# Where the rows of the other view are fetched, where the 4-bit pieces stand, and where the final copy is issued

## What is computed

```python
x = x + _L0_attn_ref(_layernorm(x, axis=-1), L0_attn_weight_qkv, L0_attn_weight_out)
x = x + _L0_xattn_ref(_layernorm(x, axis=-1), ctx_2048, L0_xattn_Wq, L0_xattn_Wk, L0_xattn_Wv)
x = x + _L0_ffn_ref(_layernorm(x, axis=-1), L0_ffn_weight1, L0_ffn_weight2, L0_ffn_weight3)
...
x = x + _L3_ffn_ref(_layernorm(x, axis=-1), L3_ffn_gate_w, L3_ffn_w1, L3_ffn_w2, L3_ffn_w3)
return x
```

## Time and profile before

| | us |
|---|---|
| Median of 3 runs (lowest, highest) | 2310.97 (2307.03, 2313.88) |
| The profiled execution, its own time | 2306.32 |
| Its span in the trace | 2304.5 |
| attn0's PE work ends, xattn0's begins | 145.9, 150.3 |
| ffn0's PE work begins | 329.5 |
| Last indirect DMA of ffn3 issued | 2287.26 |
| Final copy issued | 2295.96 |

### The profile page before, as it was taken

How to read it: one execution, slowest core, us unless ns; L and a number is a source line. 1 busy time by engine, 2 the same in 40 slices (tenths; PEclk the granted TensorE clock), 3 DMA queues, 4 the chain that set the end, 5 groups by cost and what they waited for, 6 DMA issues and landing times. The chain is left out here.

```text
span 2304.5 us, 46693 instructions
## 1 busy us (share of the span) xinstructions
PE 2055.2 (89%) x18816; PEld 1569.9 (68%) x18816; DVE 1600.1 (69%) x2975; ACT 1238.0 (54%) x2456; POOL 302.9 (13%) x307
## 2 busy tenths in 40 slices
PE   7978989899899898888889998979889779999996
PEld 4654458677555787566656666768656658999996
DVE  5756657677465897888857877857566676766763
ACT  2325664545476444555546547655478524665653
POOL 0010000011310000010000000000100113444432
PEclk9979999999999999999989999999899879999998
DMA  3020010100100002000020000010200035667663
GB/s 121 22 66 23 14 44 1 37 1 1 60 20 25 11 1 73 1 1 1 1 81 1 9 18 0 0 37 1 73 2 2 15 112 185 211 194 222 195 208 89
DMA packets 59688, 125.70 MB, mean 55 GB/s; under 512 B 12968, under 2 KB 42281, under 8 KB 59337
## 3 DMA queue, kind: packets, MB, share of 16 engines
q1 hardware_dynamic: 50666, 110.96, 14.2%
q0 software_dynamic: 8832, 12.06, 2.5%
HBM read 108.79 MB, written 15.80 MB: 54 GB/s over the span
## 5 line engine op out<-in xcount | busy, mean ns | idle before, releaser
L268 PE MATMUL ps<-ffn_xh,ffn_wh 128*128 128x256 f32 x644 | 184.1, 286 | 1.5 <-DVE ffn_xl L4388 1.5
L268 PE MATMUL ps<-ffn_xh,ffn_wl 128*128 128x256 f32 x644 | 182.2, 283 | 0.0
L268 PE MATMUL ps<-ffn_xl,ffn_wh 128*128 128x256 f32 x644 | 182.1, 283 | 0.0
L4383 DVE TENSOR_TENSOR ffn_wl<-ffn_fresh,ffn_wh 128x1792 fp32r<-128x1792 f32 x69 | 139.4, 2023 | 26.5 <-ACT ffn_wh L4263 26.5
L216 POOL TENSOR_TENSOR all_rstd<-all_mv,all_cst 128x4 f32<-128x4 f32 x40 | 8.5, 212 | 1060.8 <-DVE all_mv L194 1060.8
L1981 DVE SCALAR_TENSOR_TENSOR attn_xc<-attn_cx,all_w,attn_xc 128x512 f32<-128x512 f32 (+1 forms) x144 | 107.0, 749 | 40.2 <-ACT attn_xc L1832 36.8
L4263 ACT ACTIVATE ffn_wh<-ffn_fresh 128x1792 fp32r<-128x1792 f32 x69 | 116.9, 1695 | 14.6 <-DMA ffn_fresh<-in_l3f_w 14.6
L268 PEld LDWEIGHTS ps<-ffn_xh,ffn_wh 128*128 128x128 f32 x644 | 123.4, 192 | 1.7 <-DVE ffn_xl L4388 1.7
L268 PEld LDWEIGHTS ps<-ffn_xl,ffn_wh 128*128 128x128 f32 x644 | 123.5, 192 | 0.0
L268 PEld LDWEIGHTS ps<-ffn_xh,ffn_wl 128*128 128x128 f32 x644 | 123.4, 192 | 0.0
L3037 ACT ACTIVATE xattn_sc<-xattn_sc,xattn_mx 128x128 f32<-128x128 f32 x256 | 98.8, 391 | 17.7 <-DVE xattn_mx L3135 17.7
(11 more groups left out here) (486 smaller groups left out, 6065.6 us busy)
## 6 DMA issues: line engine op xcount, KB each, us to landing
ffn_fresh<-in_l3f_w SPq DMA_DIRECT2D x69, 896.0 KB, 4.9
all_w<-in_ctxT SPq DMA_DIRECT2D x12, 512.0 KB, 5.6
all_w<-in_ctx SPq DMA_DIRECT2D x8, 512.0 KB, 6.9
all_x<-in_x_rows SPq DMA_DIRECT2D x4, 512.0 KB, 7.4
all_x<-x_seq SPq DMA_DIRECT2D x4, 512.0 KB, 5.4
all_w<-in_l2x_o SPq DMA_DIRECT2D x1, 2048.0 KB, 9.4
xattn_ctxT<-in_ctxT SPq DMA_DIRECT2D x4, 512.0 KB, 3.8
all_w<-in_l2f_up SPq DMA_DIRECT2D x1, 2048.0 KB, 11.3
```

The costliest lines, as they stand in the source:

```text
L268: last = pe.matmul(out, a, b, start=start and n == 0, stop=stop and n == 2)
L4383: dve.tensor_tensor(wl[:, j % 2, piece(q)], fresh[:, piece(q)], wh[:, j % 2, piece(q)].bitcast(F32), ALU.subtract).then_inc(low_ready.sem, 1)
```

## The change

Four edits, in four places.

1. The wait for `x_stored` and the four fetching DMAs leave attn0's SP function and become the first steps of xattn0's SP function, ahead of `after(sp)`.
2. attn0 runs its pieces only for q < 14: 28 pieces, not 32. `DONE` becomes 19, so xattn0 has 29 pieces, 0 to 28. They are dealt by u: 2, 1, 0, 1, 2, 0, 0, 1 in the first three groups of iterations (7 pieces each, 21 in all) and 2 in each iteration of the last, which runs out of them at m = 27.
3. The two idle products at the front of xattn0's PE function are gone.
4. The copy to the output is issued by ffn3's SP function, once `added` has reached its last value, and ffn3's SP waits for it; the thirteenth Block is gone.

```diff
@@ attn0, sync @@
-            sp.wait_ge(*k.x_stored(0, 16 * (GROUPS + 2)))
-            for g in range(GROUPS):
-                at = slice(g * TG, (g + 1) * TG)
-                sp.dma_start(k.x[:, at, :], k.seq_batches[:, at, :]).then_inc(k.x_back.sem, 16)
-
@@ attn0, vector @@
-                k.nf4.beside_attn0(dve, 2 * q)
+                if q < BATCH - 2:
+                    k.nf4.beside_attn0(dve, 2 * q)
                 if q + 1 < BATCH:
                     turn_probs(q + 1)
                 divide(q)
-                k.nf4.beside_attn0(dve, 2 * q + 1)
+                if q < BATCH - 2:
+                    k.nf4.beside_attn0(dve, 2 * q + 1)
@@ xattn0, sync @@
+            sp.wait_ge(*k.x_stored(0, 16 * (GROUPS + 2)))
+            for g in range(GROUPS):
+                at = slice(g * TG, (g + 1) * TG)
+                sp.dma_start(k.x[:, at, :], k.seq_batches[:, at, :]).then_inc(k.x_back.sem, 16)
             after(sp)
@@ xattn0, vector @@
-                k.nf4.beside_xattn0(dve, m)
+                for _ in range(k.nf4.PIECES_AT[u] if g < GROUPS else 2):
+                    k.nf4.beside_xattn0(dve, pieces)
+                    pieces += 1
@@ xattn0, tensor @@
-            idle_products(pe, k, 0, 2)
             pe.wait_ge(*own)
@@ class Nf4 @@
-    DONE = 32 - 6 - 3
+    DONE = 2 * (BATCH - 2) - 6 - 3
+    PIECES_AT = (2, 1, 0, 1, 2, 0, 0, 1)
@@ ffn3, sync @@
             after(sp)
+            sp.wait_ge(*added(0, 32 * BLOCKS))
+            sp.dma_start(k.final, acc[0:ROWS, :].rearrange("(a r) d -> a (r d)", r=P // 8)).then_inc(copied_out.sem, 16)
+            sp.wait_ge(*copied_out(0, 16))
@@ build @@
-        k.phase, k.phase_ctx = "all", ctx
-        with nc.Block() as block:
-            @block.sync
-            def _(sp):
-                sp.dma_start(out.rearrange("b p d -> b (p d)").rearrange("b (q n) -> (b q) n", q=8),
-                             k.x_acc[0:ROWS, :].rearrange("(a r) d -> a (r d)", r=P // 8)).then_inc(x_out.sem, 16)
-                sp.wait_ge(*x_out(0, 16))
```

More of the change, by code:

```diff
@@ L868, in _ @@
             norm.vector(dve, 1)
+            pieces = 0
             for m in range(GROUPS * U):
@@ L1278 @@
     AT = 2048
-    SLOTS = BATCH * 2
     SUM_AT = 7
@@ L4199, in phase_ffn3 @@
     added = Signal(k, "added")
+    copied_out = Signal(k, "copied_out")
     def piece(q):
@@ L4553, in build @@
         k.x_back = Signal(k, "x_back")
-        x_out = Signal(k, "x_out")
+        k.final = out.rearrange("b p d -> b (p d)").rearrange("b (q n) -> (b q) n", q=8)
         k.nf4 = Nf4(k, k.arena(0))
```

## The result

| | us |
|---|---|
| Before: median of 7 runs (lowest, highest) | 2310.97 (2305.37, 2316.56) |
| After: median of 7 runs (lowest, highest) | 2301.05 (2295.52, 2307.93) |
| Ratio of the runs, 95% interval | 0.996 [0.9944, 0.9976] |
| The profiled execution after, its own time and span | 2305.11, 2303.3 |

The time is the forecast's to within a microsecond, but two of its three terms are not. The seam gave nothing, the group changes gave twice what was forecast, and the end gave what was forecast. "Seam" is the passage from attn0 to xattn0, a "turn" is the transposes of the normalized rows, and a "group change" is the passage from one group of four batches to the next.

A forecast was written before the change was run, and what follows sets the result against it. No engine is full over the whole span; who waits last at each place decides an edit's worth. Seam 3.4, group changes 2.5 and end 4.9 sum to 10.8 us, from the median 2310.97 to 2300.2 us; range 2292 to 2308.

The forecast's parts named there:

- The seam: Passage from attn0 to xattn0: queries start at 162.5 instead of 165.96, 3.4 us gained, bounds -1.5 to 7.
- the group changes: xattn0, groups 2 and 3: the norm starts 1.24 us sooner at each, 2.5 us gained, bounds 0 and 3.4.
- the end: Final copy after ffn3: issued at 2291.0 instead of 2295.96, 4.9 us gained, bounds 0.4 and 5.1.
- The store and the fetches keep their times: Seam: moved behind the meeting, they take as long as before, less 0.25; last landing at 156.9.
- the price of the queries: Seam: eight queries took 5.37 us, partly slow; at 0.45 or 0.86 each, 3.6 or 6.9, so 1.8 either way.
- attn0's tail: End of attn0: the sum of batch 13 starts 0.25 us sooner; bounds 0 and PE's wait of 0.85.
- The cover for the two double pieces: xattn0: two pieces delay the queries' third scale, but the fourth waits for ACT anyway; cost 0, 0.98 us to spare.
- The queries ran slow: Rival, seam: after PE's longer idle all eight queries take 6.9 us instead of 5.4; 2301.7 us; chance 0.10.
- The closing counts: Rival, end: what fills the 4.6 us must precede the copy or follow its landing; gain 0.4, 2304.7 us; chance 0.12.
- the norm's gain doesn't arrive: Rival, xattn0's group changes: turns wait for something just behind the rows; total gain 8.3, 2302.7 us; chance 0.12.
- the fetch lands early: Rival, seam: the fetch lands early, 1.8 us more gained there; 2298.4 us; chance 0.10.
- The clock stays low through keys and values: Rival, seam: TensorE's clock does not rise there, so the seam gains nothing; total gain 7.4, 2303.6 us; chance 0.13.

The follow-up runs named there:

- the warm turn: The changed kernel with six idle products of 128x512 put ahead of xattn0's first turn; 2292.46 us against 2307.71 for the kernel before, ratio 0.9925.

## Why the prediction came out right, and where it was wrong

**The seam, 3.4 forecast, -0.6 in the traces, 0 in the timed run of its own.** Its first steps held: keys at 146.9 forecast and 147.02 measured; sums at 155.5 and 155.62, so the slow start of the keys had the price I gave it. Two steps failed. The first is "The store and the fetches keep their times": the issues took 2.99 us and not 1.74 in the new place, and the last landing came at 158.9 instead of 156.9, which is 2.0 us. The second is the price of the queries, which the sum put at nothing, with 1.8 us either way in its bounds. I had the mechanism as a rival at 0.10 and it was the case, and the turn came on top: 1.94 + 6.33 against 1.04 + 5.37 is 1.9 us. Together they are the 4 us that the term was off. The row that should have decided it was in my own working: PE idle from 157.2 to 161. With 2.56 us ahead of them the queries had already run partly at 0.50.

The rule named there (the Trainium skill, "TensorE: Matmul & The Clock Gate", section "Loop structure matters more than you think") is borne out by this case: behind holes of 2.8 us and more ahead of the turn the queries took 5.7 to 6.6 us in four kernels; where the longest idle ahead of turn or queries was 1.7 or less, 3.67 in all three traces; at 2.56 it was 3.67 or 5.37. That it was the idle, and not something else at this place, the warm turn shows: with work in the hole the queries took 3.67.

**attn0's tail, 0.25 forecast.** PE's wait for the sum of batch 13 fell from 0.85 to 0.61 us: 0.24.

**The group changes, 2.5 forecast, 5.2 measured.** The step "1.24 us sooner, and PE's idle of 1.71 falls to 0.47" held to the hundredth. The bound of 3.4 was wrong, because it counted only the idle time and not what ran slow behind it: the 1.09 us of the turn stood in the earlier trace rows with nothing to explain it. The cover for the two double pieces held: the third scale ended in time, and the fourth still waits for ACT, 0.78 us instead of 0.91. In the last group batch 13's finish starts at 317.54, and `back` of batch 14 finds it done at 320.01: nothing lost, as taken.

**The end, 4.9 forecast, 4.8 in the traces and 5.1 in the timed run.** The copy left 3.71 us after the last add's issue; the closing was hidden, and its rival is out.

**The sum.** -0.6 + 5.2 + 4.8 = 9.4 us, which with the medians' 9.9 is as close as the runs allow. 10.8 was right by luck: one error of 4 us and one of 2.7 had opposite signs. The second of them and half of the first are the same omission: a hole in TensorE's work has two prices, the idle time and the speed of what follows. The other half of the first is the late landing.

**The rivals.** The queries ran slow: yes. The closing counts, the norm's gain doesn't arrive, the fetch lands early: no. The clock stays low through keys and values: in the keys alone (5.31 against 3.60), as in the forecast.

**The signs.** Those of being right all came, though the term of the seam was wrong: the keys started 0.44 us after the last store's issue had ended, the fetches left at 147.97, the norm started with their landing, and the idle ahead of the turns was 0.47. They looked at when work starts and not at how long it then takes. Of the signs of being wrong the last one came at the seam, where the granted clock was 0.50 from 162 to 170; behind it, at the group changes, it was higher than before.

## What to carry to other kernels

Cost a hole in TensorE's work twice: the idle time, and the rows behind it at the clock they then get; two like rows of different length behind an idle (1.09 and 0.67 us here) are the sign. Idle products that look like waste may be what keeps a later stage fast: before removing them, ask whether the engine then arrives early at a wait, and if so keep them, or move them to that wait; here the two served alike. And a transfer whose last part nobody needs yet may deserve a semaphore for the first part: it gave the two shortest seams here, but the one kernel with it that was timed did not show the gain.

## What the runs showed that I had not expected

The Block that ends with indirect adds takes about 4.6 us to close after the last of them has landed, 4.55 of them in GpSimd's DRAIN, and a second border behind it costs 0.2 to 0.4 us. One of four plain DMA issues at the start of a new program took 1.1 to 1.7 us on SP, in all nine traces that have them there, and 0.43 at most at the end of the old one; the cause is open. And the same kernel has a shorter seam when TensorE enters it slow (31.55 against 33.41 us), because slow products fill the hole that fast ones leave; it gives this back in the first group, where the clock falls later.
